# A mixture-of-experts stage on Trainium2: products for two blocks each, weight copies shared out anew, fewer waits of GpSimd

## The reference, cut to what matters

```python
x = x + attention(layernorm(x))          # 16 heads of 64, softmax over 256 keys, output product and bias
x = x + ffn(layernorm(x))

# ffn, on all 4096 tokens
probs = sigmoid(x @ router_w.T + expert_bias)            # 160 experts
top_w, top_idx = top_k(probs, 8)
top_w = 2.5 * top_w / (sum(top_w) + 1e-09)
h1 = silu(x @ w_gate[e].T)                               # 64 hidden values per expert
routed = sum over the 8 chosen e of top_w[e] * (h1 @ w_down[e].T)
shared = silu(x @ w_gate_shared.T) @ w_down_shared.T     # an expert that every token uses
out = routed + shared
```

## Time and profile before

| | |
|---|---|
| median of 3 runs | 1049.58 us |
| the profiled execution's own time | 1049.12 us |
| its span (first to last instruction) | 1047.3 us |
| busy: PE, ACT, DVE, POOL | 82%, 74%, 71%, 67% |
| TensorE's mean granted clock | 0.923 of 2.4 GHz |
| group work (first gate to last output) | 649.6 to 959.4 us |
| gathers | 714.1 to 1041.6 us |

### The profile page before, as it was taken

One profiled execution on the slowest core, in us unless ns is written; L12 is line 12 of the kernel. 1 busy time (PEld: TensorE's weight loads), 2 busy tenths in 40 slices (PEclk: granted clock), 3 DMA queues, 4 the chain that ended last, 5 costly groups with the idle time before them and its releaser, 6 DMA issues.

```text
span 1047.3 us, 30540 instructions
## 1 busy us (share of the span) xinstructions
PE 860.7 (82%) x8800; PEld 664.1 (63%) x8800; DVE 741.7 (71%) x2514; ACT 770.5 (74%) x2408; POOL 704.8 (67%) x884
## 2 busy tenths in 40 slices
PE   6999999999999999999999997898787766664000
PEld 5777777777777777777777775676565544443000
DVE  5568888888878868888888888777476555554223
ACT  6888888888888878888888887779999755565000
POOL 3235676677677666776776776635777777777775
PEclk9999999999999999999999999899999877788555
DMA  8915654444443311221221224688888766665221
GB/s 239 381 47 227 250 209 158 169 167 185 171 172 146 110 68 63 87 91 63 82 96 60 78 101 165 212 293 264 275 270 262 226 192 197 185 203 164 58 59 52
DMA packets 75993, 169.99 MB, mean 162 GB/s; under 512 B 13856, under 2 KB 24416, under 8 KB 75936
## 3 DMA queue, kind: packets, MB, share of 16 engines
q1 hardware_dynamic: 57248, 133.63, 36.3%
q0 software_dynamic: 16384, 33.59, 11.2%
q10 hardware_dynamic: 2304, 2.10, 0.6%
HBM read 66.50 MB, written 102.76 MB: 162 GB/s over the span
## 4 chain that ended last, share of the span: by engine, by line
PE 44%; POOL 18%; issue 13%; DVE 12%; ACT 6%; DMA 3%; DVEq 1%; ACTq 1%; POOLq 0%; SPq 0%
POOL yg L990 15%; PE psS L454 10%; PE psO L532 8%; PE psT L482 7%; PE psY L445 6%; PE psA L494 4%; PE psVM L445 3%; ACT p_sb L758 3%; DVE negmax L1314 2%; DVE w_b L1355 2%; DMA block_y<-y_b 2%; ACT w_b L834 1%; PE psS L643 1%; POOL slot_x L963 1%; ACTq L272 1%
## 5 line engine op out<-in xcount | busy, mean ns | idle before, releaser
L990 POOL DMA_INDIRECT yg<-block_y,pos_u x256 | 249.7, 975 | 100.7 <-issue 74.7
L963 POOL DMA_INDIRECT slot_x<-xn_src,slot_u x240 | 244.7, 1020 | 95.7 <-issue 53.5
L758 ACT ACTIVATE p_sb<-psS,negmax 128x256 f32<-128x256 f32 x512 | 236.1, 474 | 99.1 <-DVE negmax L1314 98.7
L925 POOL TENSOR_SCALAR p_sb<-p_sb,rinv 128x256 f32<-128x256 f32 x256 | 142.6, 565 | 117.3 <-DVE rinv L1263 113.7
L1314 DVE TENSOR_REDUCE negmax<-psS 128x2 f32<-128x512 f32 x256 | 164.1, 682 | 28.0 <-PE psS L454 27.7
L454 PE MATMUL psS<-qk_sb 64*128 64x256 f32 x1024 | 145.6, 403 | 2.3 <-ACT p_sb L758 2.3
L321 ACT COPY pT_sb<-psT 128x512 f32<-128x512 f32 x256 | 140.9, 617 | 4.3 <-PE psT L482 4.3
L532 PE MATMUL psO<-pT_sb,v_sb 128*64 128x256 f32 x1024 | 138.8, 391 | 1.6 <-ACT pT_sb L321 1.1
L482 PE MATMUL psT<-ident,p_sb 128*128 128x128 f32 x1024 | 133.5, 274 | 2.3 <-POOL p_sb L925 2.3
L1355 DVE COPY w_b<-w_all 128x192 f32 x497 | 104.6, 276 | 41.8 <-issue 20.8
L643 PE MATMUL psS<-xbT,w_b 128*64 128x64 f32 x1664 | 76.9, 239 | 57.0 <-DVE w_b L1355 38.0
(11 more groups left out here) (181 smaller groups left out, 1879.5 us busy)
## 6 DMA issues: line engine op xcount, KB each, us to landing
block_y<-zero SPq DMA_DIRECT2D x26, 1024.0 KB
xb<-slot_x SPq DMA_DIRECT2D x104, 256.0 KB
block_y<-y_b SPq DMA_DIRECT2D x96, 256.0 KB
slot_x<-zero SPq DMA_DIRECT2D x15, 1024.0 KB
w_all<-in_wgd_dram SPq DMA_DIRECT2D x16, 960.0 KB, 4.8
slot_x<-zero SPq DMA_DIRECT2D x1, 11264.0 KB, 41.5
yg<-block_y,pos_u POOLq DMA_INDIRECT x256, 2.4
slot_x<-xn_src,slot_u POOLq DMA_INDIRECT x240
```

The source lines that it names most:

```text
L758: act.activation(p_sb[:, (g - 1) % 2, h, qt, :], psS[:, h, qt * SEQ:(qt + 1) * SEQ], ACT.Exp, bias=negmax[:, (g - 1) % 2, h, qt:qt + 1], s ...
L925: pool.tensor_scalar(pq, pq, rinv[:, (g - 2) % 2, k // 2, k % 2:k % 2 + 1], 1.0, ALU.mult, ALU.mult).then_inc(s["pn_ok"], 1)
L963: pool.indirect_dma_start(slot_x, bass.IndirectOffsetOnAxis(ap=slot_u[:, int(last), i, j:j + 1], axis=0), (xn2 if last else xn2_src)[:, i, ...
L990: pool.indirect_dma_start(yg[:, r, k, :], None, block_y, bass.IndirectOffsetOnAxis(ap=pos_u[:, n, k:k + 1], axis=0)).then_inc(gat_last if ...
```

## The change

Two blocks now share one place in the weight ring: the last dimensions of `w_b` are (pair of blocks, 3 pieces, 2 blocks, 64), so that the gate weights of both lie side by side and likewise each half of the down weights. Every copy of a block's 192 values therefore writes three pieces of 64 with a gap of 64 between them, in all 104 groups and on both engines.

From group 40 on (`JOINT_FROM`) `gates` makes four products of 128 stationary columns (both experts) by 128 moving columns (both blocks' rows), and `downs` four products with 128 stationary columns (both blocks' hidden values, 64 rows deep) by 256 moving columns (both experts' down weights). Of each product only the two diagonal quarters are used. `silu` and `outputs` therefore read them with two and four instructions of 64 partitions, where they had one and two of 128.

VectorE copies all eight blocks' weights in groups 28 to 39 too, where it copied four, and six of eight from group 40 on, where it copied four; ScalarE copies the rest. From gather 48 on GpSimd waits for the transposes at every sixth gather, not at every third; the values waited for are as before.

```diff
@@ -40,8 +40,8 @@
 RW = GB * HB // P
 RING = 4
 YR = 4
-W_EARLY, W_LATE = 5, 4
-ACT_EARLY, ACT_LATE = 7, 28
+W_EARLY, W_LATE = 5, 6
+ACT_EARLY, ACT_LATE = 7, 40
 E_LATE = 20
 
 
@@ -51,10 +51,12 @@
 FRESH = E + SEALED * SEQ_BLK
 
 COMBINE_FROM = 10
+JOINT_FROM = RING * COMBINE_FROM
 STORE_LAG = 6
 WIDE_FROM, WIDE_TO = 2 * RING, (E + SEQ_BLK) // GB
 STATE_AT = 4 * E
-PACE, PACE_HEAD, PACE_FROM = 3, 27, 33
+PACE, PACE_LATE, PACE_APART, PACE_HEAD, PACE_FROM = 3, 6, 48, 27, 33
+JOINT = (0, 1, 4, 5)
 NGRP = NBLK // GB
 CLEAR = NBLK * HB // 1024
 CLEAR_A = 22
@@ -229,7 +231,7 @@
         xbT = sb("xbT", [D, 2, RW, P])
         h_b = sb("h_b", [P, 2, GB // 2, HB])
         y_b = sb("y_b", [P, 2, RW, D])
-        w_b = sb("w_b", [P, RING, GB, INTER + D])
+        w_b = sb("w_b", [P, RING, GB // 2, 1 + D // INTER, 2, INTER])
         xb = sb("xb", [P, RING, RW, D])
         blk_i = sb("blk_i", [P, NBLK], I32)
         w_all = sb("w_all", [P, E, INTER + D])
@@ -277,6 +279,22 @@
         def is_wide(n):
 
             return WIDE_FROM <= n < WIDE_TO
+
+        def pair_of(i):
+
+            return i % 2 + 2 * (i // 4), i // 2 % 2
+
+        def weights_at(r, i):
+
+            c, h = pair_of(i)
+            return w_b[:, RING - 1 - r, c, :, h, :]
+
+        def weights_from(e):
+            return w_all[:, bass.ds(e, 1), :].rearrange("p o (k i) -> p (o k) i", i=INTER)
+
+        def is_joint(n, share):
+
+            return n >= JOINT_FROM if isinstance(n, int) else share
 
         def y_at(r, wide):
 
@@ -618,6 +636,7 @@
 
 
             hidden = h_b[:].rearrange("p a k t -> p a (k t)")
+            rows_of = xbT[:].rearrange("p a k (i t) -> p a i k t", i=GB)
 
             def hidden_place(i):
                 c = i % 2 + 2 * (i // 4)
@@ -638,21 +657,33 @@
                 if share and copied_by_dve(n) < GB:
                     pe.wait_ge(s["wa_cp"], act_copies(n) + 1)
                 wait(pe, s["h_ok"], n - 1)
-                for i in TILES:
+                for i in JOINT if is_joint(n, share) else ():
+
+                    c, _ = pair_of(i)
+                    m = pe.matmul(psS[:, par, c * 2 * HB:(c + 1) * 2 * HB],
+                                  w_b[:, RING - 1 - r, c, 0].rearrange("p h i -> p (h i)"),
+                                  rows_of[:, par, i:i + 3:2], start=True, stop=True)
+                for i in () if is_joint(n, share) else TILES:
                     half, cols = hidden_place(i)
-                    m = pe.matmul(psS[half, par, cols], w_b[:, RING - 1 - r, i, 0:INTER],
+                    m = pe.matmul(psS[half, par, cols], weights_at(r, i)[:, 0],
                                   xbT[:, par, :, i * P // GB:(i + 1) * P // GB], start=True, stop=True)
                 m.then_inc(s["g_ps"], 1)
 
-            def downs(r, n):
+            def downs(r, n, share=True):
                 par = r % 2
                 ps = ((psY, psVM), (psO, psA))[par]
                 wait_apart(pe, s["y_ok"], n - 1)
                 wait_apart(pe, s["h_ok"], n + 1)
-                for i in TILES:
+                for i in (0, 2, 4, 6) if is_joint(n, share) else ():
+
+                    k, j = i // 2 % 2, i // 4
+                    half = slice(k * INTER, (k + 1) * INTER)
+                    m = pe.matmul(ps[k][:, 0, j * 2 * D:(j + 1) * 2 * D], hidden[half, par, j * 2 * HB:(j + 1) * 2 * HB],
+                                  w_b[half, RING - 1 - r, 2 * j:2 * j + 2, 1:, k, :], start=True, stop=True)
+                for i in () if is_joint(n, share) else TILES:
                     half, cols = hidden_place(i)
                     m = pe.matmul(ps[i // 2 % 2][i % 2 * HB:(i % 2 + 1) * HB, 0, i // 4 * D:(i // 4 + 1) * D],
-                                  hidden[half, par, cols], w_b[half, RING - 1 - r, i, INTER:], start=True, stop=True)
+                                  hidden[half, par, cols], weights_at(r, i)[half, 1:], start=True, stop=True)
                 m.then_inc(s["y_ps"], 1)
 
             def experts(it, chunk=None, share=True):
@@ -695,7 +726,7 @@
                     if early == 3:
                         pe.wait_ge(s["ot_ok"], NSTEP)
                         pe.wait_ge(s["x1_ok"], B)
-                    downs((r - 2) % RING, n - 2)
+                    downs((r - 2) % RING, n - 2, share)
 
             pe.wait_ge(s["pt0_ok"], NSTEP)
             pe.wait_ge(s["pt1_ok"], NSTEP)
@@ -796,19 +827,25 @@
                 wait(act, s["g_ps"], n - 1)
                 act.copy(xbT[:, par].rearrange("p a t -> p (a t)"), psT[:, par, :]).then_inc(s["xt2_ok"], 1)
 
-            def silu(r, n):
+            def silu(r, n, share=True):
                 par = r % 2
                 act.wait_ge(s["g_ps"], n + 1)
                 wait(act, s["y_ps"], n - 1)
-                act.activation(h_b[:, par].rearrange("p k t -> p (k t)"), psS[:, par, 0:GB // 2 * HB],
-                               ACT.Silu).then_inc(s["h_ok"], 1)
+                for h in range(2) if is_joint(n, share) else ():
+
+                    half = slice(h * INTER, (h + 1) * INTER)
+                    m = act.activation(h_b[half, par], psS[half, par, :].rearrange("p (k h t) -> p k h t", h=2, t=HB)[:, :, h, :],
+                                       ACT.Silu)
+                if not is_joint(n, share):
+                    m = act.activation(h_b[:, par].rearrange("p k t -> p (k t)"), psS[:, par, 0:GB // 2 * HB], ACT.Silu)
+                m.then_inc(s["h_ok"], 1)
 
             def stored(r, n, back):
 
                 c = (r - back) % RING
                 act.wait_ge(sty[c], 16 // RING * (n - back - c) + 16)
 
-            def outputs(r, n, wide=False):
+            def outputs(r, n, wide=False, share=True):
                 par = r % 2
                 act.wait_ge(s["y_ps"], n + 1)
                 if not isinstance(n, int):
@@ -823,7 +860,12 @@
                     act.wait_ge(s["lg_ps"], B)
                     act.wait_ge(s["x2_st"], 16 * B)
                 y = y_at(r, is_wide(n) if isinstance(n, int) else wide)
-                for k in range(2):
+                for k, h in [(k, h) for k in range(2) for h in range(2)] if is_joint(n, share) else []:
+
+                    half = slice(h * HB, (h + 1) * HB)
+                    m = act.copy(y[half, k::2, :], ((psY, psVM), (psO, psA))[par][k][half, 0, :].rearrange(
+                        "p (a h d) -> p a h d", h=2, d=D)[:, :, h, :])
+                for k in () if is_joint(n, share) else range(2):
                     m = act.copy(y[:, k::2, :], ((psY, psVM), (psO, psA))[par][k][:, 0, 0:RW // 2 * D].rearrange("p (a d) -> p a d", d=D))
                 m.then_inc(s["y_ok"], 1)
 
@@ -831,7 +873,7 @@
 
                 first = copied_by_dve(n)
                 for i, e in enumerate(experts_of(act, n, first, GB - first), first):
-                    m = act.copy(w_b[:, RING - 1 - r, i, :], w_all[:, bass.ds(e, 1), :].rearrange("p o i -> p (o i)"))
+                    m = act.copy(weights_at(r, i), weights_from(e))
                 m.then_inc(s["wa_cp"], 1)
 
             def experts(it, chunk=None, share=True, wide=False):
@@ -851,21 +893,21 @@
                         keep_input(B)
                         weights_of(2, 2)
                         exponentials(B)
-                    silu((r - 1) % RING, n - 1)
+                    silu((r - 1) % RING, n - 1, share)
                     if r == 0 and chunk is not None:
                         shared(chunk)
                     if early == 1:
                         weights_of(3, 3)
                         continue
-                    outputs((r - 2) % RING, n - 2, wide)
+                    outputs((r - 2) % RING, n - 2, wide, share)
                     if share and (early is None or early + 2 < NGRP and copied_by_dve(early + 2) < GB):
                         weights_of((r + 2) % RING, n + 2)
 
             for it in range(LEAD):
                 experts(it)
-            with act.Fori(LEAD, ACT_LATE // RING - 1) as it:
+            with act.Fori(LEAD, WIDE_TO // RING) as it:
                 experts(it, share=False, wide=True)
-            for it in range(ACT_LATE // RING - 1, COMBINE_FROM - 1):
+            for it in range(WIDE_TO // RING, COMBINE_FROM - 1):
                 experts(it)
             act.wait_ge(s["tab_ok"], 2)
             experts(COMBINE_FROM - 1, 0)
@@ -985,7 +1027,7 @@
                 for k in range(TOPK):
 
                     i = TOPK * n + k
-                    if i % PACE == 0:
+                    if i % (PACE if i < PACE_APART else PACE_LATE) == 0:
                         pool.wait_ge(s["xt2_ps"], min(PACE_HEAD + i // 2, PACE_FROM + i // PACE, NGRP))
                     pool.indirect_dma_start(yg[:, r, k, :], None, block_y,
                                             bass.IndirectOffsetOnAxis(ap=pos_u[:, n, k:k + 1], axis=0)
@@ -1352,7 +1394,7 @@
                 if not first:
                     dve.wait_ge(s["y_ps"], n - RING + 1)
                 for i, e in enumerate(chosen_experts):
```

(2 more changed lines are left out.)

## The result

The changed kernel takes 1067.8 us (median of four runs, 1066.8 to 1072.0), where the one before took 1049.4 beside it: ratio 1.0176, 95% interval 1.0154 to 1.0198. The forecast was 1053.7, its range 1045 to 1060. It is slower by 18 us. The share of a part is the difference of two such ratios, times 1050 us; each of the two is known to some 3 us only.

A forecast was written before the change was run, and what follows sets the result against it. GpSimd's gathers, 1.25 us each, were taken as the bound. First gather +3.6, groups 28 to 39 +1.5, joint products 0, GpSimd's waits 0, longer gathers -1.0 and +0.5: +4.6 on 1049.1, so 1053.7 us, range 1045 to 1060.

The forecast's parts named there:

- The bound: GpSimd's 256 gathers at 1.25 us each; only a later first gather, longer gathers or GpSimd waits cost time.
- The copies' price: VectorE weight copies into three runs go at full price per element: 0.27 us apart, 340 to 360 ns; 7 in 10.
- The first gather: Longer VectorE copies in the groups up to 24 delay GpSimd's first gather: +3.6 us, ends +1.5 and +7.
- Groups 28 to 39: VectorE making all eight copies runs some 7 us late by group 39, against some 5 of slack: +1.5 us.
- the slack of 5.8: Time between the end of group 35's transposes (731.02) and the gather at 736.85 that needs them: 5.8 us.
- Joint products: Paired gates and downs from group 40: every engine below 3.75 us a group, hidden by GpSimd, 0.
- ScalarE's 2.7 us a group: ScalarE's cycle from group 40: 2.28 us, +0.95 for three more instructions, -0.51 for two copies fewer.
- GpSimd's waits: Every second wait dropped from gather 48 on; they end nothing today and the 0.30 us gap stays: 0.
- Longer gathers: Gathers stretched by VectorE: copies no longer stretch them, -1.0 us; combines with a busier VectorE, +0.5 (ends -5 and +6).
- (a): Rival: weight copies keep their price, the start stays; 1049.7 us, between 1047 and 1052; chance 0.25.
- (b): Rival: GpSimd waits in groups 30 to 47, VectorE keeping its pauses at 3.0 us a group; 1060 us; chance 0.17.
- (c): Rival: gathers lose their stretched cases as combines fall beside the beat; 1042 to 1047, say 1044 us; chance 0.13.

The follow-up runs named there:

- r1: The changed kernel with each weight copy walked as two halves of 96 elements on both engines: 1062.9 us, ratio 1.0113 to the kernel before.
- t1: The kernel before with the interleaved weight ring and the combines of tiles 0 and 1 one turn earlier: 1050.5 us, ratio 1.0003.
- v1: The kernel before with two of eight weight copies on ScalarE also in groups 7 to 27, and TensorE's wait for them: 1050.1 us, ratio 0.9997.
- u1: The changed kernel with VectorE and ScalarE copying four blocks each in groups 28 to 39, as before: 1058.9 us, ratio 1.0097.
- s1: The changed kernel with single gate and down products for one block each, as before: 1061.7 us, ratio 1.0132.
- r4: The changed kernel with copies walked in two halves and the old shares (ScalarE four of eight copies from group 28): 1077.7 us, ratio 1.0256.
- s3: The kernel before with GpSimd waiting for the transposes every sixth gather from gather 48 on: 1048.4 us, ratio 0.9994.
- u2: The changed kernel with four copies each in groups 28 to 39 and the combines of tiles 0 and 1 one turn earlier: 1056.6 us, ratio 1.0073.
- s2: The changed kernel with a group's four output copies ordered both lower halves first, then both upper: 1070.3 us, ratio 1.0202.
- t2: The changed kernel with output copies ordered lower halves first and the combines of tiles 0 and 1 one turn earlier: 1064.8 us, ratio 1.0134.
- run 254: Not a follow-up run: a VectorE copy of 192 elements written as one contiguous run takes 254 ns.
- r2: The kernel before with the interleaved weight ring alone (single products, old shares): 1053.3 us, ratio 1.0034.

## Why the prediction was wrong, by its own steps

The forecast was +4.6 us, and the two steps that failed are the work of groups 28 to 39, put at +1.5, and the joint products, put at 0; of the 16.4 us of waits in the profile after, 9.5 are for the reuse of `yg`, for which the sum has no term.

**The bound** was read rightly: 1.25 us a gather before and after, and all lost time is a later first gather, a longer gather or a wait of GpSimd, nearly all of it between gathers 12 and 47, as it said.

**The copies' price** (0.27 apart, 340 to 360 ns): right, 0.26 and 342. By the rule cited from the Trainium skill (page "VectorE: DVE Perf Modes", section "What auto-detection actually checks") three pieces lose the mode; r1, with two even outermost dimensions, has 253 ns back, so the trace agrees.

**The first gather** (+3.6): too high, by the step that let the longer copies show in groups 7 to 24. They fill the pauses (90 without a gap, 2.09 a group against 2.11), t1 costs nothing (under 2 us by its interval), and in v1 less work on VectorE gave nothing. The +5.2 of the profile after is no evidence: the nine kernels with the dear copy started between 713.5 and 719.3, those with the cheap one between 712.2 and 718.6. A small cost of 1 or 2 us is not excluded.

**Groups 28 to 39** (+1.5): the largest error; taking this part out (u1) gives back 8 us. The step "12.5 + 8.4 = 21 us of work, 6 us later than today and some 7 by group 39" was short: in s1 the copies of group 34 start 9.5 us later than before (738.53 for 729.05), those of group 39 10.0 (749.26 for 739.21), as pauses of 0.6 to 1.0 us stay where routing work stands between. Its transposes of group 35 end 11.0 us later (742.06 for 731.02); less the slack of 5.8, rightly read, that is 5.2, and gather 18 of s1 waits 5.3 with its ordinary 0.3. The second slack was never read: gathers 32 and 40 wait for combines of VectorE, and had 1.8 and 2.3 us.

**Joint products** (0, "below 3.75"): wrong twice. ScalarE's 2.7 us a group was mis-sized, it is 3.42: the three more instructions, put at 0.95 us, came to 1.52, as the two silus and four outputs stand 0.38 apart, where one silu and two outputs stood 0.25 to 0.28 apart; and two copies left take 0.63, not 0.51. And 3.75 is the mean over turns with 1.5 combines, while behind the first turn stands one: there a group may take 2.5 us, and up to gather 64 3.3. "Were that cover gone, 0.4 us of ACT times 64 groups would be 28 us" came out in r4, which lost 27, by another size: 4.24 a group is 0.49 over 3.75.

**GpSimd's waits** (0): right, s3. But "the reuse of `yg` still waits for the combine" named the very wait that carries more than half of the lost time, and gave it no slack.

**Longer gathers** (-1.0 and +0.5): the first part right, the second too small. Of the gathers that ran beside copies, and beside no product of a combine, 7 to 17 in each of the seven traces with cheap copies took 0.97 us or more (12 in the one before, 0.5 to 1.0 us in sum), and not one did in the nine traces with dear copies, where the longest took 0.96. By the Trainium skill (page "SBUF — State Buffer", section "Who interferes with whom") copies out of the two-port mode should spare GpSimd; these traces agree. The gathers that take 1.15 us or more nearly all lie under a product of a combine: before 12 of them, 6.4 us in sum, in the change 13 and 8.3, so +1.9 for the forecast +0.5. In all the gathers are 1.2 us longer (9.0 for 7.8), and over the kernels r1 to u2 this sum lies between 5.7 and 13.3, by how the combines fall.

**Rivals.** (a) fell with the price. (b), GpSimd waiting in groups 30 to 47 at 1060, had the right place; s1, the change without the joint work, took 1061.7. But its reason, that VectorE keeps its pauses and needs 3.0 us a group, was wrong in the main: groups 34 to 38 run without one at 2.10 us a group, and pauses of 0.6 to 1.0 us stand only in the groups among the last routing work. (c) did not occur.

Still open: what sets the first gather (in v1 TensorE and ScalarE are busy 14.1 and 14.3 of 16 us ahead of it, and the stores were not tried apart), and why ScalarE's 0.2 us a group less in s2 and t2 gave no time; in both traces more gathers lie under a product of a combine (16 and 19, in the change 13).

## What to carry to other kernels

Before a cost is called hidden, list every wait of the bounding engine that has ended early, the reuse of its buffers too, and read the slack of each from the trace; the smallest one, here 1.8 us, decides, and several parts of a change can draw on it together. A mean rate that is allowed (3.75 us) hides nothing at the start of a phase, where the order of the work may ask for a higher one (2.5). A moved share is priced on the engine that gets it with everything queued behind it.

## What the runs showed of the hardware

- ScalarE starts an instruction on 64 partitions 0.27 us after the last if both use the same half, and 0.38 after it if the half changes (s2); full-width ones of the same row length follow each other after 0.25 to 0.28 (before). So a full-width instruction split in two costs 0.76 for some 0.27.
- Joining products of 64 columns cost TensorE time: gates 1.06 us for 0.69, downs 1.13 for some 0.67, at a granted clock of 1.00 both times. Single products run beside each other: in the trace of before two downs on different halves start at 727.77 and 727.78, both 0.32 us long.
- A VectorE copy of 192 elements in three runs takes 342 to 346 ns, as two even halves 253, in one run 254. ScalarE's price did not change with the shape: a copy takes 368 ns in the mean before and in r2, and four take 1.12 us before and 1.11 in r4.
- A VectorE copy at 254 ns stretches a gather of GpSimd beside it to 0.97 us and up to some 1.04 now and then, one at 342 ns never did (1012 gathers beside such copies, the longest 0.96). A combine's product of 1024 elements stretches one to as much as 2.0 us.
- One chip took 13 to 14% longer with every kernel tried on it; output copies were held there up to 24 us after the issue of the store that they wait for.
